# Linear attention and distance output computed for both batches at once, linear inputs loaded a stage early, q softmax in two parts, later fetches in distance attention

## The reference, cut to what matters

```python
# linear attention: R = 2 batches, C = 1025 tokens, 8 heads; heads are formed by reshaping (8, C, 16)
q, k, v = (to_heads(x @ W.T + b) for W, b in ((Wq, bq), (Wk, bk), (Wv, bv)))
q = softmax(q, axis=-1) * 4
k = softmax(k, axis=-2)
out = q @ (k.T @ v)                  # per head; k.T @ v is a 16 x 16 context
h = h + out
...
# distance attention: q, k, v of 255 selected tokens, 8 heads
attn = -scale * sum(abs(q[:, None] - k[:, :, None]), axis=-1)
b = softmax(attn, axis=1) @ v        # then summed over heads and scattered back to the tokens
...
# distance output
y = bsum * sigmoid(1.702 * bsum)
h = xn + fanout_w(y)                 # linear layer with a bias; plus the residual
```

## Time and profile before

| what | value |
|---|---|
| median of 3 runs | 1448.46 us (1448.35 to 1449.5) |
| the profiled execution's own time | 1447.95 us |
| its span in the trace | 1446.2 us |
| linear stage | 269 to 325 us of the span |
| distance attention, its 128 steps | 1021.8 to about 1302 us |
| distance output | 1309.5 to 1335.5 us |
| PE, DVE, ACT, POOL busy | 77%, 62%, 53%, 10% of the span |

### The profile page before, as it was taken

One profiled execution on the slowest core, in us unless ns is written; L12 is line 12 of the kernel. 1 busy time (PEld: TensorE's weight loads), 2 busy tenths in 40 slices (PEclk: granted clock), 3 DMA queues, 4 the chain that ended last, 5 costly groups with the idle time before them and its releaser, 6 DMA issues. The chain is left out here.

```text
span 1446.2 us, 27934 instructions
## 1 busy us (share of the span) xinstructions
PE 1110.9 (77%) x11498; PEld 648.6 (45%) x11498; DVE 892.9 (62%) x1929; ACT 769.1 (53%) x1076; POOL 141.1 (10%) x159
## 2 busy tenths in 40 slices
PE   6667955382778979955999999979899999997240
PEld 3456944381534444441333333365444555667220
DVE  0476457647891177765675555564777979953624
ACT  0451323121207643348999999922687978962020
POOL 0006302202001200000000000010000000001424
PEclk9778987555557979956999999969899999995575
DMA  6100000022000000000000000010000000002021
GB/s 143 28 1 1 4 4 9 7 30 46 3 1 1 1 0 1 1 2 3 1 2 1 2 1 1 2 39 1 2 2 2 2 2 2 2 2 66 12 45 27
DMA packets 42315, 18.18 MB, mean 13 GB/s; under 512 B 37504, under 2 KB 41138, under 8 KB 41934
## 3 DMA queue, kind: packets, MB, share of 16 engines
q1 hardware_dynamic: 40462, 15.32, 5.0%
q0 software_dynamic: 1728, 1.08, 0.4%
HBM read 12.88 MB, written 3.48 MB: 11 GB/s over the span
## 5 line engine op out<-in xcount | busy, mean ns | idle before, releaser
L2398 ACT ACTIVATE pt_PT<-ps 128x1024 f32<-128x1024 f32 x288 | 266.1, 1111 | 5.8 <-PE ps L2468 5.4
L3417 ACT ACTIVATE da_AD<-ps,da_NX 128x1024 f32<-128x1024 f32 x214 | 222.4, 1123 | 41.0 <-PE ps L3498 40.4
L3498 PE MATMUL ps<-da_AD,dw_win 128*32 128x256 f32 x4080 | 230.7, 380 | 8.9 <-DVE da_AD L3369 8.9
L3369 DVE TENSOR_SCALAR da_AD<-da_QH,da_XG,da_XH 128x1024 f32<-128x1024 f32 x296 | 217.5, 811 | 13.8 <-PE ps L3498 13.4
L3498 PEld LDWEIGHTS ps<-da_AD,dw_win 128*32 128x32 f32 x4080 | 128.0, 110 | 108.2 <-DVE da_AD L3369 19.8
L2434 PE MATMUL ps<-pt_PT,pa_V 128*32 128x512 f32 (+3 forms) x1536 | 154.9, 497 | 8.3 <-DVE pt_Yc L2375 3.2
L2382 DVE TENSOR_TENSOR pt_PT<-pt_PT,pt_keep 128x512 f32<-128x512 f32 x128 | 84.3, 690 | 61.5 <-ACT pt_PT L2398 60.3
L2468 PE MATMUL ps<-pt_QT,pt_KT 12*128 12x512 bf16 (+3 forms) x768 | 80.3, 334 | 3.4 <-DVE pt_KT L2340 0.5
L2434 PEld LDWEIGHTS ps<-pt_PT,pa_V 128*32 128x32 f32 x1536 | 38.8, 109 | 64.5 <-issue 63.3
L2007 ACT ACTIVATE mt_act<-ps 128x342 f32<-128x342 f32 (+1 forms) x66 | 30.1, 455 | 54.0 <-PE ps L2062 54.0
L2062 PE MATMUL ps<-mt_XF,ew_w 64*128 64x342 f32 (+1 forms) x132 | 54.2, 494 | 0.9 <-ACT mt_WT L1993 0.8
(11 more groups left out here) (766 smaller groups left out, 2098.7 us busy)
## 6 DMA issues: line engine op xcount, KB each, us to landing
em_xs<-in_x_dram SPq DMA_DIRECT2D x2, 1152.0 KB, 9.2
em_xs<-in_x_dram SPq DMA_DIRECT2D x2, 1024.0 KB, 13.5
cp_xbuf<-ci_zero SPq DMA_DIRECT2D x1, 672.0 KB
cp_XS<-cp_xbuf SPq DMA_DIRECT2D x8, 84.0 KB, 2.2
cp_ybuf<-cp_YS SPq DMA_DIRECT2D x8, 84.0 KB, 2.1
ew_win<-in_L_ffn_w_dram SPq DMA_DIRECT2D x2, 320.0 KB
em_WS<-in_L_tok_W_dram SPq DMA_DIRECT2D x8, 72.0 KB
la_blk<-la_scratch SPq DMA_DIRECT2D x8, 64.1 KB
```

The costliest lines, as they stand in the source:

```text
L2398: nc.scalar.activation(PT[:, n % RING, 2 * i:2 * i + 2, :], ps[:, b0:b0 + 2, :], ACT.Exp, scale=SCALE).then_inc(exp_ok, 1)
L3369: nc.vector.tensor_scalar(AD[:, j % RING], QH[:, b], XG[:, b, s:s + 1], XH[:, b, s:s + 1], ALU.max, ALU.subtract).then_inc(ad_dve, 1)
L3417: nc.scalar.activation(AD[:, j % RING], QA, ACT.Abs, bias=NX[:, b, s:s + 1]).then_inc(ad_act, 1)
L3498: ins = nc.tensor.matmul(o, D.win[:, int(by[j] == "D"), hp, 15 - m:47 - m], AD[:, j % RING, hp], start=False, stop=m == (14 if (k, q) == ( ...
```

## The change

A class `LinearInputs` owns the linear stage's weights, biases and constants. Its 14 loads and 4 memsets are issued in the depths stage, behind that stage's own loads on SP and ahead of the masks on POOL. In the linear stage, both batches now lie side by side in 128 partitions (`la_x2`, `la_XT` of 128 partitions); the weights are in a block form of 128x128 (`WT`), and one matmul serves both batches. The bias comes by matmuls of its own (`bias_q`, `bias_kv`, N=512 or 384 with all 128 rows) that open the accumulation in each bank. The last step of the layernorm is in three parts. The softmax of q is made for tiles 0 to 3 and 4 to 8 apart, and the store is in two parts too. In distance attention the fetches stand four steps behind PE's step, the `weigh` products five steps apart. The distance output is done for both batches at once in the same manner (`f2` is the block form, `fb` the bias).

```diff
+def stage_linear(nc, K, A):
+    with ExitStack() as ctx:
+        I = LinearInputs(K, ctx)
+        depths(nc, K, A, I)
+        linear_attention(nc, K, A, I)
...
+                I.load(sp, A)
...
                 nc.gpsimd.memset(ones[:], 1.0).then_inc(ones_ok, 1)
+                I.fill(nc, pool)
...
+                sp.wait_ge(q_ok, 1)
+                sp.dma_start(tiles(0, EARLY), q[:, 0:EARLY]).then_inc(stored, 16)
+                sp.wait_ge(q_ok, 2)
+                sp.dma_start(tiles(EARLY, 8), q[:, EARLY:8]).then_inc(stored2, 16)
+                sp.dma_start(scratch[8192:8208].rearrange("(p h) e -> p (h e)", h=H), q[7:9, 8]).then_inc(stored2, 16)
+                sp.wait_ge(stored, 16)
+                for g in range(EARLY - 1):
+                    load(g)
+                sp.wait_ge(stored2, 32)
+                for g in range(EARLY - 1, H):
+                    load(g)
...
-                layernorm_dve(nc, dve, link, K.h[:], xn[:], tmp[:], st[:], var_ready, std_ready)
+                for g in range(3):
+                    s = slice(3 * g, 3 * g + 3)
+                    tt(x2[:].rearrange("p i b d -> p b i d")[:, :, s], by_batch(xn[:])[:, :, s],
+                       rstd[:, :, s].unsqueeze(3).to_broadcast([P, B, 3, 64]), ALU.mult).then_inc(x_ok, 1)
...
+                for a in range(2):
+                    dve.wait_ge(q_sb, (1, 3)[a])
+                    link(nc.vector.tensor_reduce(qs[:, 0, of[a]], q3[a], AX.X, ALU.max))
+                    tt(q3[a], q3[a], bcl(qs[:, 0, of[a]], 16), ALU.subtract).then_inc(qd_ok, 1)
...
+                def whole(a):
+                    dve.wait_ge(qe_ok, a + 1)
+                    link(nc.vector.tensor_reduce(qs[:, 1, of[a]], q3[a], AX.X, ALU.add))
+                    link(nc.vector.reciprocal(qs[:, 2, of[a]], qs[:, 1, of[a]]))
+                    tt(q3[a], q3[a], bcl(qs[:, 2, of[a]], 16), ALU.mult).then_inc(q_ok, 1)
...
-                bring(0)
-                act.wait_ge(qd_ok, 1)
-                nc.scalar.activation(q[:], q[:], ACT.Exp).then_inc(qe_ok, 1)
-                for i in range(1, 4):
+                for a in range(2):
+                    act.wait_ge(qd_ok, a + 1)
+                    nc.scalar.activation(q[:, PART[a]], q[:, PART[a]], ACT.Exp).then_inc(qe_ok, 1)
+                for i in range(4):
                     bring(i)
...
+                def bias_kv(bank):
+                    nc.tensor.matmul(ps[:, bank, :].rearrange("p (g c) -> p g c", g=2), lone[:],
+                                     bc(wb[:, 1:3].rearrange("p a c -> p (a c)"), 2), start=True, stop=False,
+                                     skip_group_check=True)
...
-    XFIRST, XEVERY, XLAG = 2, 4, 1
+    XFIRST, XEVERY, XLAG = 2, 4, 4
...
-    WEIGH = {68 + 2 * hp: hp for hp in range(4)}
+    WEIGH = {68 + 5 * hp: hp for hp in range(4)}
+    EXPS = {16 * e + (27 if e == 4 else 19): e for e in range(7)}
...
-                        if n - 1 in WEIGH:
-                            gather(WEIGH[n - 1])
+                        if n - XLAG in WEIGH:
+                            gather(WEIGH[n - XLAG])
...
-                    nc.gpsimd.memset(YT[64:65], 1.0).then_inc(one_ok, 1)
```

## The result

The changed kernel takes 1409.87 us, the median of 4 runs (1408.72 to 1412.94), where the kernel before, on the same chip, takes 1448.98 (1448.35 to 1455.94, 4 runs). The ratio is 0.972, with a 95% interval of 0.969 to 0.976. The forecast was 1412.5, in a range of 1406 to 1424. The profiled execution took 1408.72 us, 39.2 less than that of before.

The account below looks back on a forecast made before the run. PE was taken to bound distance attention, and two nearly equal paths hanging on PE's products the linear stage. Linear -13.7, attention -8.9, output -13.7 and switch +0.3 gave -36.0 us, to 1412.5, range 1406 to 1424.

Parts of the forecast that it names:

- The sum: Whole kernel: linear -13.7, attention -8.9, output -13.7, switch stage +0.3, together -36.0 us, to 1412.5; chance 0.50.
- Linear stage, -13.7: Linear stage: `la_blk` 13.8 us earlier, `la_cx` just ahead of it, the end as before, so -13.7 us.
- The q path: Linear stage, x through q's softmax to stores and loads: q 11.9 us earlier, first load at 289.1.
- with 14.1 us from the first load to the last landing: Linear stage: the eight unchanged loads take 14.1 us as before, so `la_blk` is there at 303.7.
- my two nearly equal paths: Linear stage before: q's path to PE's turn at 317.52 and the context's to `la_cx` at 318.59 were nearly equal.
- the queue behind the second store: Linear stage: the loads queue behind q's second store, adding 0.5 us before `la_blk` is there.
- The rival on the early loads: Linear stage: early loads do nothing, as the old ones landed before x was ready; counted inside the low-clock rival.
- Attention, -8.9: Distance attention: with four steps of lead DVE keeps up and PE's 12 waits for it vanish, -8.9 us.
- no more than 8.9, since PE is busy otherwise: Distance attention: upper bound of the gain, 8.9 us, PE having no other idle time to lose.
- Output, -13.7: Distance output: 36 records of N=128 instead of 72, clock up after 4.5 us, stage end 1335.5 to 1321.8, -13.7 us.
- my rival: Distance output: clock stays at 1.2 GHz throughout, only -7.6 us, total 1418.6; low clock in one stage 0.20.
- The other cases: Low clock in one changed stage 0.20, both 0.08; attention's stalls move 0.12; slower, attention's clock lowered, 0.02.

Follow-up runs that it names:

- the whole softmax: Changed kernel with q's softmax and its store in one part over all nine tiles; linear stage 42.59 us.
- the memset: Changed kernel with one more POOL memset of 1x2052 elements in the linear stage, into a row nobody reads; linear stage 39.61 us.
- no biases: Changed kernel without the bias products of q, k and v; linear stage 39.89 us.
- the early fetches: Changed kernel with distance attention's fetches one step behind again, not four; steps 284.07 us, run 1409.3 us.
- The runs with eight and with four stops: Changed kernel with fetches one step behind (eight), or weighted sums two steps apart, their gathers one behind (four); steps 284.07 and 279.97 us, runs 1409.3 and 1410.2.
- second profile of the same kernel: The changed kernel run once more, without edits, beside a version with dummy products; 1410.27 us, ratio 0.974.
- the run with attention alone: Kernel before with only the four edits of distance attention (fetches, weighted sums, gathers, fifth Exp); 1429.79 us, ratio 0.986.
- The narrow run: Changed kernel with the distance output's scatter again in 72 records of N=64, not 36 of N=128; output stage 25.44 us.
- the kept-busy run: Changed kernel with dummy products wherever PE stands idle near the linear stage, attention's set-up and the output; 1408.44 us, ratio 0.972.

## Why the prediction was right, point by point

**The sum** came out 2.6 us too high, 3.2 for the profiled execution (1411.95 against 1408.72). Two gains were each some 3 us larger than forecast, linear and the steps, and the switch stage took 0.5 us less. The set-up (+1.6) and the rest (+1.0), both put at 0, and the output (+0.5) went the other way. So the mechanisms were right in the main, but that the total came this close is in part luck: errors that had nothing to do with each other offset by half. I had also put the resolution at 0.2% (2.9 us); the changed kernel's ten runs went from 1403.28 to 1416.96.

**Linear stage, -13.7 against -16.56.** The q path went nearly as worked out: first load 19.1 us into the stage (20.1 forecast). The step that failed is "with 14.1 us from the first load to the last landing". The row behind it, the transposition at 317.52, had no wait for a DMA ahead of it but PE's own work, and the DMA engines had gone quiet 2.1 us earlier (timeline of PE, then windows with the DMA share last but one, before):
```profile
314.08 3.60 PE L1342 MATMUL ps<-la_R,la_fold 128*128 128x17 f32 x16
```
```profile
303.40:315.40 12.00, 8.90 (x38) 7.64 (x37) 7.39 (x18) 2.09 (x5) 0.00 (x0) 0.50 0.47 44
315.40:317.50 2.10, 2.10 (x11) 2.10 (x12) 0.00 (x0) 0.00 (x0) 0.00 (x0) 0.50 0.00 0
```
It stood behind the fold products, so the 14.1 us were PE's order and only a bound for the landing; my two nearly equal paths were one path, the context's, and another with some 1.5 us to spare. Where PE did wait for la_blk, in the runs with the whole softmax, the memset, no biases and the early fetches, it was 12.4, 12.7, 12.6 and 12.5 us. In the changed kernel la_blk was turned at 304.00, 12.6 us behind the first load and right behind the fold products; by those runs it was landed between 303.8 and 304.1. So the two paths tied within 0.3 us, PE shows no wait between them, and `la_cx` was done 1.5 us earlier into the stage than I had it. Of the 3.0 us by which la_blk was turned earlier than forecast, 1.5 is this term, 1.0 the earlier first load, and 0.5 the queue behind the second store, which did not show. The earlier first load is the second missed term, DVE's step beside POOL's memset, 1.2 us: the change took the memset out, and I had called LayerNorm "the same". The clock rose 5.4 us after the first bias product, not 4.5, which took a little of it back. The depths stage kept its 44.3 us, so the early loads and fills cost nothing there, as forecast.

**The rival on the early loads** was wrong by 10 us, and my sentence that the old ones were landed before x was ready did not see that 14 loads now stand where 8 did, that the biases stand ahead of x, and that ACT's copy of the weights stands ahead of LayerNorm's root.

**Attention, -8.9 against -11.87 in the steps.** The mechanism was right, four steps are lead enough, and DVE keeps up. The step that failed is "no more than 8.9, since PE is busy otherwise": busy time held another 3.0 to 3.6 us. The runs with eight and with four stops bear the size out, about 0.3 us a stop. The set-up's +1.6 came with the clock's fall at the stage's start (the sum of the 36 records at its start took 5.88 us, 4.26 in the run with attention alone) and was not there in the second profile of the same kernel.

**Output, -13.7 against -13.18.** Right, scatter 6.61 for 6.3, clock up 5.0 us after PE's start for 4.5. The narrow run shows what most of the gain hangs on: with all the rest in the new form the stage took 25.44, so 12.5 us came with the wide scatter. At one and the same clock of 1.00 it was worth 3.2; the rest is the clock, which rose in the wide scatter and not in the narrow one. That the shape is the reason is borne out by this place only (eight profiles against three); elsewhere in the same traces it is not. At 0.50 throughout, the stage would have been 7.6 us shorter by my rival; no run had that.

**The other cases.** No clock stayed low in a changed stage, no stall moved, and nothing slowed attention's clock (0.99 as before).

**The rest, +1.0**, are single stages with unchanged code that moved by up to 3.6 us. The largest one, in windows of before, after, and of the second profile of the changed kernel:
```profile
618.40:664.50 46.10, 16.08 (x58) 14.79 (x58) 33.63 (x51) 29.14 (x59) 2.05 (x2) 0.51 0.01 2
```
```profile
604.15:646.64 42.49, 10.22 (x58) 9.24 (x58) 33.52 (x51) 29.08 (x58) 2.01 (x2) 0.64 0.01 2
```
```profile
598.95:645.03 46.08, 16.07 (x58) 14.79 (x58) 33.60 (x52) 29.19 (x58) 2.01 (x2) 0.51 0.01 2
```
The same 58 records on PE take 10.2 or 16.1 us as the clock rises in time for them or not. So part of any single difference between two profiles here, by these rows up to 3 or 4 us a stage, is no effect of an edit. What decides the moment of the rise stays open.

## What to carry to other kernels

Before a gap between a DMA's issue and its first reader is taken as the transfer's time, look whether the reader was waiting: if its engine was busy until then, the gap is only an upper bound. Idle time listed for PE understates what a stop costs, here by 0.3 us a stop, or three to four tenths of what is listed. And where a stage is paced by small matmuls, count its records at both clocks and look at what raises the clock ahead of it; judge an edit by its own stretch in the trace, since the other stages move by more than a small edit is worth.

## What the runs showed of the hardware

- In the output's scatter 72 records with 114 weight columns and N=64 left the clock at 0.50 for 14.15 us of unbroken work in three profiles of three, while 36 with N=128 had it at 1.00 after 3.7 to 5.0 us in eight of eight. Once it was up, the narrow ones kept it at 1.00 for 7.38 us.
- The shape alone does not decide: 10.4 us of wider forms behind a narrow scatter stayed at 0.50, and in the linear stage of the run with attention alone the clock rose in narrow transpositions and fell 3.4 us later in narrow products, with PE busy for the last 2.4 us. The Trainium skill ("TensorE: Matmul & The Clock Gate", Why this matters for your kernels) has the clock rise with unbroken work and fall after a pause: the 14.15 us disagree, and so do that fall and the one at 1295.2 in the kept-busy run, with PE busy since 1288.0.
- The moment of the clock's rise moved stages with unchanged code by 2.8, 3.2 and 3.6 us between runs (PE's busy time by 2.8, 3.2 and 5.9).
- A POOL memset of one partition and 2052 elements (1.80 us) held a DVE `tensor_scalar` of 18 columns for 1.13 us (0.18 without).
- A stop of PE costs about 0.3 us more than its listed idle time (3.6 us for 12, 2.5 for 8, 0.9 for 4).
